# First attention of a two-layer gated block: sums over keys by a block of ones, the pair divided ahead of one 128-row output product

## The chip, the cores and the metric

The kernel runs on one core of a Trainium2 chip. The metric is the device time of one execution in microseconds (us), from start to end; of several runs the median is taken. The engines are named as in the profile: PE (TensorE, with PEld for its weight loads), DVE (VectorE), ACT (ScalarE), POOL (GpSimd) and SP (SyncE). A name like L713 is a line of the kernel before.

## The reference

Two layers, each an attention to a context of 77 rows and a feed-forward part. The change touches the first attention alone: queries come from the 2 x 1024 normalized rows of x (the latents), keys and values from the 77 rows of the context and from those rows themselves, 1101 keys in all, with 4 heads of 64.

```python
def _L0_xattn_ref(x, latents, mask, ...):        # x: the context, latents: layernorm of x
    xn, ln = layernorm(x, ...), layernorm(latents, ...)
    q = ln @ W_q
    kv = concatenate([xn @ W_kv, ln @ W_kv], axis=1)
    ...
    qn = rmsnorm(q, q_gamma) * SCALE
    kn = rmsnorm(k, k_gamma)
    sim = einsum('bhid,bhjd->bhij', qn, kn)
    sim = where(full_mask[:, None, None, :], sim, neg)
    attn = softmax(sim, axis=-1)
    out = einsum('bhij,bhjd->bhid', attn, v)
    out = out.transpose(0, 2, 1, 3).reshape(b, nl, INNER)
    return out @ W_out + b_out
...
x = x + tanh(g_xattn[0]) * _L0_xattn_ref(ctx_1024, _layernorm(x, axis=-1), mask_BxS2_bk0, ...)
x = x + tanh(g_ffn[0]) * _L0_ffn_ref(...)
x = x + tanh(g_xattn[1]) * _L1_xattn_ref(...)
x = x + tanh(g_ffn[1]) * _L1_ffn_ref(...)
```

## The kernel before

Every engine has its own program, written out by hand in `layers_kernel`; semaphores join them. The stages stand one after the other: weights of the second attention folded, the first projection, the first attention (97 to 407 us of the span), the spiking feed-forward part, the second attention, routing and experts. All data is 32-bit.

**Pairs and steps.** The first attention goes over 8 *pairs* (`PP`; 0 to 7), each two heads by 512 query rows of one batch: pairs 0 to 3 are batch 0, pairs 4 to 7 batch 1. A pair has 9 *steps* c, one for each chunk of 128 keys (the last of 77). In a step `pe_attend` puts out, in this order: `key_scores` (L713, L714: scores with keys as rows, for both heads, into banks 3 and 4), one `row_scores` of the *next* pair (L689, whose largest value DVE takes by `row_max`, L830), some small pieces, and `values` (L722) of those chunks that `CHUNK_OF_STEP` gives to the step. ACT takes the exponentials of the key scores into `EX`, a ring of four chunks (L1022). The row maxima of a pair are turned by `turn_shift` (L703) and copied by `keep_shift` (L849) into a row of the queries, so that the next pair's scores come out shifted.

**The end of a pair.** POOL adds the exponentials of the first six chunks (L986), DVE the others and both sums (`sum_first`, `sum_rest`, L858 to L866) into `sumD`. In step 1 of the next pair `sums` (L731) adds `sumD` over its 128 rows: eight products whose moving side is one column of ones, so that the sums of 128 queries come out on 128 rows, one column each. `reciprocals` (L870) inverts those 8 columns. ACT has copied the unscaled output to `OT`, 64 rows a head. `project_out` (L742), one half in step 2 and one in step 4, multiplies OT with W_out, head by head, since each head has its own divisor; `add_out` (L885) scales each head's product by its column and adds it to X, eight operations of 256 columns in a pair.

**Pieces.** While pairs 1 to 4 run, the projections of the other heads (two *units* of 9 items, first for pairs 4 and 5, then for pairs 6 and 7) are made beside them: `item` (L759), DVE's `square_sums` and `scale_heads` (L903, L914) with POOL's root between (L994), `turn_heads` (L768), ACT's copies and DVE's `low_parts_of` (L927, L930). The tables FIRST_AT, FIRST_TURNS (pairs 1 and 3), SECOND_AT, SECOND_TURNS (pairs 2 and 4), ROWS_AT and NORM_AT give each piece its step. What DVE does of an item or a turn beyond the square sums stands at the start of its next step. `keys_there` (step 0 of pairs 3 and 5) holds the next pair's row scores until the last piece of its unit is through.

**Spare banks.** All small products share banks 2, 6 and 7. `spare_uses` lists the uses in the order in which PE comes to them, and the k-th use takes bank k % 3, so a use waits until the use three places before it has been read:

```python
    def open_bank(pe, *use):
        k = order_of[use]
        if k >= 3:
            pe.wait_ge(bank_free[k % 3], k // 3)
        return SPARE[k % 3]
```

## Time and profile before

| what | value |
|---|---|
| median of 3 runs | 935.12 us (933.39 to 937.04) |
| profiled execution, its own time | 933.5 us |
| its span, first to last instruction | 931.1 us |
| mean granted clock of TensorE | 0.935 |
| busy over the span: PE, PEld, DVE | 845.8, 626.1, 607.6 us |
| busy over the span: ACT, POOL | 313.8, 372.8 us |

The profile is of one execution; its windows and starts count from its first instruction. A product of two 32-bit operands stands in the trace as two records (`x`). The granted clock is a share of the full one: 1.00 is 2.4 GHz, 0.50 is 1.2 GHz. A matmul's end is modelled, and the next begins before it; where a price matters, it is read from a run of like products. A wait put down to "issue" is one for which the profile shows no releaser. `DVEq L888` is the empty instruction by which `add_out` gives a bank free.

### The profile page before, as it was taken

To read this page: it belongs to the slowest core of one execution; us is meant where nothing else is said; L and a number is where in the kernel's file an instruction comes from. 1 tells how busy PE (TensorE), PEld (TensorE's weight loads), DVE (VectorE), ACT (ScalarE), POOL (GpSimd) and SP (SyncE) were. 2 spreads that over 40 slices of the span, in tenths; PEclk is the share of its full clock that TensorE was granted. 3 is DMA by queue.
4 is the path that set the end of the run, shared out by engine and by line. 5 is a ranking of instruction groups with operands and counts; after the bars stand their busy time and mean duration, and the time that the engine had idled before them with its cause. 6 is when DMAs were issued, how large, how long until landed. Compare 5 with 4: busy or idle time off the path is not lost.

```text
span 931.1 us, 13492 instructions
## 1 busy us (share of the span) xinstructions
PE 845.8 (91%) x4334; PEld 626.1 (67%) x4335; DVE 607.6 (65%) x1199; ACT 313.8 (34%) x703; POOL 372.8 (40%) x389
## 2 busy tenths in 40 slices
PE   6888799999999899969999799999997889999995
PEld 5455445555655555448888577777776779999994
DVE  5959676776677576359988688899886723333331
ACT  4557134543445233423444122333331022222220
POOL 4255555362556264524447044434443313222221
PEclk9999599998999799969999899999999799999999
DMA  8381000000000000045000650000000274555530
GB/s 304 119 313 49 1 1 0 1 1 1 1 0 1 1 0 1 2 147 211 0 0 1 205 167 8 12 12 12 13 11 18 77 262 159 175 188 188 167 85 2
DMA packets 32135, 67.88 MB, mean 73 GB/s; under 512 B 3161, under 2 KB 23095, under 8 KB 30999
## 3 DMA queue, kind: packets, MB, share of 16 engines
q1 hardware_dynamic: 28887, 56.63, 17.6%
q0 software_dynamic: 2624, 10.49, 3.7%
q8 instruction: 24, 0.39, 0.2%
q10 hardware_dynamic: 578, 0.18, 0.1%
q14 instruction: 22, 0.18, 0.1%
HBM read 55.20 MB, written 13.01 MB: 73 GB/s over the span
## 4 chain that ended last, share of the span: by engine, by line
PE 67%; DVE 18%; issue 7%; ACT 3%; POOL 2%; DMA 2%; DVEq 0%; SPq 0%; ACTq 0%; POOLq 0%
PE PS L2047 9%; PE PS L2035 8%; PE PS L1420 7%; PE PS L1438 6%; PE PS L722 6%; PE PS L1264 4%; PE PS L713 4%; PE PS L689 3%; DVE row_best L830 3%; PE PS L714 3%; PE PS L759 2%; PE PS L1422 2%; PE PS L731 2%; PE PS L742 2%; PE PS L1248 2%
## 5 line engine op out<-in xcount | busy, mean ns | idle before, releaser
L1022 ACT ACTIVATE EX<-PS 128x512 f32<-128x512 f32 x144 | 79.1, 594 | 139.7 <-PE PS L714 134.8
L830 DVE TENSOR_REDUCE row_best<-PS 128x1 f32<-128x1024 f32 x64 | 77.8, 1221 | 49.2 <-PE PS L689 48.9
L986 POOL TENSOR_TENSOR sumP<-sumP,EX 128x1024 f32<-128x1024 f32 x32 | 75.6, 2363 | 42.4 <-ACT EX L1022 41.8
L2035 PE MATMUL PS<-xeT,w 128*128 128x128 f32 x736 | 86.1, 275 | 3.6 <-DMA w<-in_L_ffn_W 2.6
L2035 PEld LDWEIGHTS PS<-xeT,w 128*128 128x128 f32 x736 | 85.6, 192 | 5.1 <-DMA w<-in_L_ffn_W 2.8
L2047 PE MATMUL PS<-w,heT 128*128 x368 | 83.3, 379 | 1.3 <-DVE oe L1977 1.3
L722 PE MATMUL PS<-EX,V 128*64 128x512 f32 (+1 forms) x288 | 75.9, 645 | 0.0
L2047 PEld LDWEIGHTS PS<-w,heT 128*128 128x128 f32 x368 | 68.1, 190 | 10.0 <-issue 1.7
L2074 POOL DMA_INDIRECT out<-oe,target x23 | 23.2, 1011 | 127.4 <-DVE oe L1977 127.4
L1438 PE MATMUL PS<-vw,pcT 128*128 128x256 f32 (+1 forms) x320 | 73.1, 383 | 1.2 <-ACT pcT L1630 1.2
L713 PE MATMUL PS<-QA,KA 100*128 100x512 f32 x144 | 71.3, 495 | 0.6 <-ACT EX L1022 0.6
L1438 PEld LDWEIGHTS PS<-vw,pcT 128*128 128x128 f32 (+1 forms) x320 | 59.6, 190 | 9.0 <-issue 1.3
L713 PEld LDWEIGHTS PS<-QA,KA 100*128 100x128 f32 x144 | 28.9, 200 | 49.7 <-issue 38.5
L714 PE MATMUL PS<-QB,KB 128*128 128x512 f32 x144 | 61.5, 427 | 0.0
L2007 ACT ACTIVATE heT<-PS,cols 128x128 f32<-128x128 f32 x92 | 26.2, 368 | 101.8 <-PE PS L2035 101.8
L1966 DVE TENSOR_SCALAR heT<-PS,cols 128x128 f32<-128x128 f32 x92 | 25.9, 344 | 52.7 <-PE PS L2035 52.7
L689 PE MATMUL PS<-KA,QA 65*128 65x512 f32 x128 | 49.5, 477 | 11.3 <-DVE row_best L830 5.3
L1311 POOL TENSOR_TENSOR square<-relu 128x512 f32<-128x512 f32 x32 | 38.0, 1196 | 33.9 <-ACT relu L1287 33.3
L1619 ACT ACTIVATE pc<-pc 128x462 f32<-128x462 f32 (+1 forms) x32 | 22.9, 717 | 81.2 <-DVE pc L1520 81.2
L1975 DVE TENSOR_TENSOR oe<-PS,b 128x256 f32<-128x256 f32 x23 | 9.8, 424 | 61.0 <-PE PS L2047 61.0
L1675 POOL TENSOR_TENSOR pc<-pc,sum 128x462 f32<-128x462 f32 x16 | 16.8, 1049 | 66.9 <-DVE sum L1528 66.9
L689 PEld LDWEIGHTS PS<-KA,QA 65*128 65x128 f32 x128 | 27.1, 228 | 24.5 <-DVE row_best L830 12.7
(292 smaller groups left out, 1793.7 us busy)
## 6 DMA issues: line engine op xcount, KB each, us to landing
w<-in_L_ffn_W SPq DMA_DIRECT2D x31, 1024.0 KB, 6.0
vw_rows<-vwn SPq DMA_DIRECT2D x2, 1232.0 KB
kwH_rows<-kwH SPq DMA_DIRECT2D x1, 2464.0 KB
kwL_rows<-kwL SPq DMA_DIRECT2D x1, 2464.0 KB
kwH<-kwH_rows POOLq DMA_DIRECT2D x1, 2464.0 KB, 10.4
kwL<-kwL_rows POOLq DMA_DIRECT2D x1, 2464.0 KB, 14.9
vw<-vw_rows SPq DMA_DIRECT2D x2, 1152.0 KB, 7.2
XR<-in_x SPq DMA_DIRECT2D x4, 512.0 KB, 13.5
```

The lines of the kernel that those rows point to most:

```text
L689: last = pe.matmul(PS[:, at + k0 // 512, 0:k1 - k0], QA[0:MASKROW + 1, g, h, s * P:s * P + P], KA[0:MASKROW + 1, h, k0:k1], start=True, st ...
L713: pe.matmul(out, KA[0:SHIFT + GT, h, cols], QA[0:SHIFT + GT, g, h, :], start=True, stop=False)
L714: pe.matmul(out, KB[:, h, cols], QB[:, g, h, :], start=False, stop=True).then_inc(st_done, 1)
L722: last = pe.matmul(PS[i * E0:i * E0 + E0, PV_AT, :], V[0:r, c, h, :], EX[0:r, (KT * n + c) % EB, i, :], start=c == 0, stop=c == KT - 1)
L830: dve.tensor_reduce(row_best[:, n % 2, t // GT, t % GT:t % GT + 1], PSf[:, 512 * at:512 * at + S], AX.X, ALU.max, negate=True).then_inc(ma ...
L986: pool.tensor_tensor(sumP[:], before, EX[:, (KT * n + c) % EB, :, :], ALU.add).then_inc(pool_summed, 1)
L1022: act.activation(EX[0:r, k % EB, i, :], PS[0:r, ST_AT + i, :], ACT.Exp).then_inc(exp_done, 1)
L1311: pool.tensor_tensor(square[:, c % 4, :], relu[:, c % 4, :], relu[:, c % 4, :], ALU.mult).then_inc(squared, 1)
L1420: pe.matmul(PS[:, 1 + i, 0:c1 - c0], z[:, p, k * P:k * P + P], w[:, k, b, c0:c1], start=w is kwH and z is zcH and k == 0, stop=False)
L1438: ins = pe.matmul(PS[:, 7, 0:D], pcT[0:r, c, :], vw[0:r, b, c, :], start=c == 0, stop=c == HC - 1)
L2035: last = pe.matmul(PS[:, 1 + 2 * p + c // 4, c % 4 * P:c % 4 * P + P], w1[:, u, k, c * P:c * P + P], xeT[:, p, k, :], start=k == 0, stop=k ...
L2047: last = pe.matmul(PS[:, 5 + p, 0:D], heT[:, p, c, :], w[:, ds(e * (FC * D) + c * D, D)], start=c == 0, stop=c == FC - 1)
```

## The change

The sums over keys: `sums` multiplies `sumD` (moving, 512 columns) by a 128 x 64 block of ones, one product a head, so that the sum of each query stands on all 64 rows of its head, the layout of OT. `reciprocals` inverts these 512 columns in two halves, one in step 1 behind the row maximum and one in step 2, and the sums' bank is free after the second; `scale_out` multiplies OT by them into `rl`. `project_out` takes both heads in one product of 128 rows (W_out lies as 2 blocks of 128 rows, loaded by one transfer), a half in step 3 and a half in step 5, into one bank each; `add_out` is one addition of 512 columns a half. The tables move pieces of pairs 2 and 4 to earlier steps, and the second `turn_shift` goes behind the first values of step 8.

```diff
-    onecol = att.take("onecol", [P, 1])
+    ones64 = att.take("ones64", [P, E0])
...
-    wout = att.take("wout", [P, H0, D])
+    wout = att.take("wout", [P, KC, D])
...
-    SECOND_AT = {0: (4,), 2: (5,), 3: (6,), 5: (7,), 6: (8,)}
+    SECOND_AT = {0: (4,), 1: (5,), 2: (6,), 4: (7,), 5: (8,)}
...
-    SECOND_TURNS = {1: (3,), 2: (4,), 4: (5,), 5: (6,), 7: (7,), 8: (8,)}
+    SECOND_TURNS = {1: (3,), 2: (4,), 3: (5,), 4: (6,), 6: (7,), 7: (8,)}
...
             k0 = open_bank(pe, "sum", n, 0)
             pe.wait_ge(dve_summed, 3 * n + 3)
             for i in range(2):
-                for s in range(GT):
-                    last = pe.matmul(PS[:, k0, i * GT + s:i * GT + s + 1],
-                                     sumD[:, i, s * P:s * P + P], onecol[:], start=True, stop=True)
+                last = pe.matmul(PS[i * E0:i * E0 + E0, k0, :], ones64[:], sumD[:, i, :], start=True, stop=True)
             last.then_inc(sum_done, 1)

         def project_out(n, half):
-            if half == 0:
-                pe.wait_ge(ot_ready, n + 1)
-            banks = [open_bank(pe, "out", n, 2 * half + i) for i in range(2)]
+            k0 = open_bank(pe, "out", n, half)
+            pe.wait_ge(out_scaled, n + 1)
             for s in (2 * half, 2 * half + 1):
-                for i, h in enumerate(heads_of(n)):
-                    lo = slice(i * E0, i * E0 + E0)
-                    last = pe.matmul(PS[:, banks[i], s % 2 * D:s % 2 * D + D], OT[lo, n % 2, s * P:s * P + P],
-                                     wout[lo, h, :], start=True, stop=True)
+                last = pe.matmul(PS[:, k0, s % 2 * D:s % 2 * D + D], rl[:, s * P:s * P + P], wout[:, n // 2 % 2, :],
+                                 start=True, stop=True)
             last.then_inc(proj_done, 1)
...
-                    if c in (5, 8):
-                        turn_shift(n + 1, (c - 5) // 3)
+                    if c == 5:
+                        turn_shift(n + 1, 0)
...
-                    if c == 2:
+                    if c == 3:
                         project_out(n - 1, 0)
-                    if c == 4:
+                    if c == 5:
                         project_out(n - 1, 1)
...
                 for done in CHUNK_OF_STEP.get(c, ()):
+                    if done == KT - 1 and n + 1 < PP:
+                        turn_shift(n + 1, 1)
                     values(n, done)
...
-        def reciprocals(n):
+        def reciprocals(n, half):
             dve.wait_ge(sum_done, n + 1)
-            bank_read(dve.reciprocal(rl[:, n % 2].rearrange("p i s -> p (i s)"),
-                                     PS[:, bank_of("sum", n, 0), 0:2 * GT]), "sum", n, 0)
+            if n > 0:
+                dve.wait_ge(proj_done, 2 * n)
+            w = slice(half * (GN // 2), half * (GN // 2) + GN // 2)
+            ins = dve.reciprocal(rl[:, w], PS[:, bank_of("sum", n, 0), w])
+            if half == 1:
+                bank_read(ins, "sum", n, 0)
+
+        def scale_out(n):
+            dve.wait_ge(ot_ready, n + 1)
+            wait_read(dve, "sum", n, 0)
+            dve.tensor_tensor(rl[:], OT[:, n % 2, :], rl[:], ALU.mult).then_inc(out_scaled, 1)
...
-            for i in range(2):
-                for s in (2 * half, 2 * half + 1):
-                    done = 2 * GT * n + GT * half + 2 * i + s % 2
-                    if done >= 2:
-                        dve.wait_ge(proj_added, done - 1)
-                    row = X[:, batch_of(n) * (S // P) + GT * group_of(n) + s, :]
-                    ins = dve.scalar_tensor_tensor(row, PS[:, bank_of("out", n, 2 * half + i), s % 2 * D:s % 2 * D + D],
-                                                   rl[:, n % 2, i, s:s + 1], row, ALU.mult, ALU.add).then_inc(proj_added, 1)
...
+            if n >= 2:
+                wait_read(dve, "out", n - 2, half)
+            at = batch_of(n) * (S // P) + GT * group_of(n) + 2 * half
+            rows = X[:, at:at + 2, :]
+            bank_read(dve.tensor_tensor(rows, PS[:, bank_of("out", n, half), :].rearrange("p (s d) -> p s d", d=D), rows,
+                                        ALU.add), "out", n, half)
...
                 if n > 0 and c == 1:
-                    reciprocals(n - 1)
+                    reciprocals(n - 1, 0)
                 if n > 0 and c == 2:
+                    reciprocals(n - 1, 1)
+                    scale_out(n - 1)
+                if n > 0 and c == 3:
                     add_out(n - 1, 0)
-                if n > 0 and c == 4:
+                if n > 0 and c == 5:
                     add_out(n - 1, 1)
...
-        for lo in (0, E0):
-            sp.dma_start(wout[lo:lo + E0], t["L0_xattn_W_out"].rearrange("(h e) n -> e h n", e=E0)).then_inc(wts_in, 16)
+        sp.dma_start(wout[:], t["L0_xattn_W_out"].rearrange("(r p) n -> p r n", p=P)).then_inc(wts_in, 16)
```

Three places show how the order moves. In the rows of the changed kernel the lines are its own: L714, L715 key scores, L690 row scores, L723 values, L764 turned heads, L755 items, L704 the turned shift, L738 the output product.

The first place is PE in steps 1 and 2 of pair 2, from the sums of pair 1 on. Before:

```order
L731 MATMUL PS<-onecol,sumD 128x1 x8
L768 MATMUL PS<-ident,qk 128x128 x4
L722 MATMUL PS<-EX,V 64x512 x2
L713 MATMUL PS<-QA,KA 128x512
L714 MATMUL PS<-QB,KB 128x512
L713 MATMUL PS<-QA,KA 128x512
L714 MATMUL PS<-QB,KB 128x512
L689 MATMUL PS<-KA,QA 128x512 x2
L742 MATMUL PS<-wout,OT 128x256 x4
L768 MATMUL PS<-ident,qk 128x128 x4
L759 MATMUL PS<-wqkv,lnT 128x384 x2
```

Now:

```order
L731 MATMUL PS<-sumD,ones 64x512 x2
L764 MATMUL PS<-ident,qk 128x128 x4
L755 MATMUL PS<-wqkv,lnT 128x384 x2
L723 MATMUL PS<-EX,V 64x512 x2
L714 MATMUL PS<-QA,KA 128x512
L715 MATMUL PS<-QB,KB 128x512
L714 MATMUL PS<-QA,KA 128x512
L715 MATMUL PS<-QB,KB 128x512
L690 MATMUL PS<-KA,QA 128x512 x2
L764 MATMUL PS<-ident,qk 128x128 x4
L755 MATMUL PS<-wqkv,lnT 128x384 x2
```

Item 5 has come from step 2 to step 1, item 6 from step 3 to step 2, and the output product has left step 2, so that the turn of item 4 (the second L764) follows the row scores of step 2 and stands three uses of a spare bank behind the sums.

The second place is DVE in the same steps, from the scaling of item 4's heads (`qk`, bracketed is what the instruction waits for) to the first add of before, and to the scaled output now. Before:

```order
L914 TENSOR_TENSOR qk<-PS,rrms 128x512 [waits v_ready,rrms_ready]
L830 TENSOR_REDUCE row_best<-PS 128x1 [waits s_done]
L870 RECIPROCAL rl<-PS 128x8 [waits sum_done]
L896 TENSOR_SCALAR Z<-ctxn,meanvar,rstd 128x256 [waits zT_done]
L927 SCALAR_TENSOR_TENSOR QB<-PS,cols,QB 64x2x128 [waits high_ready]
L930 SCALAR_TENSOR_TENSOR KB<-PS,cols,KB 64x2x128
L830 TENSOR_REDUCE row_best<-PS 128x1 [waits s_done]
L885 SCALAR_TENSOR_TENSOR XR<-PS,rl,XR 128x256 [waits bias_added,proj_added,bank_free2,proj_done]
```

Now:

```order
L916 TENSOR_TENSOR qk<-PS,rrms 128x512 [waits v_ready,rrms_ready]
L828 TENSOR_REDUCE row_best<-PS 128x1 [waits s_done]
L871 RECIPROCAL rl<-PS 128x256 [waits proj_done,sum_done]
L905 TENSOR_REDUCE ssum<-sq 128x4 [waits sq_ready]
L908 TENSOR_SCALAR rms<-ssum 128x4 [waits ssum_ready]
L929 SCALAR_TENSOR_TENSOR QB<-PS,cols,QB 64x2x128 [waits high_ready]
L932 SCALAR_TENSOR_TENSOR KB<-PS,cols,KB 64x2x128
L916 TENSOR_TENSOR qk<-PS,rrms 128x512 [waits v_ready,rrms_ready]
L828 TENSOR_REDUCE row_best<-PS 128x1 [waits s_done]
L871 RECIPROCAL rl<-PS 128x256 [waits proj_done,sum_done]
L878 TENSOR_TENSOR rl<-OT,rl 128x512 [waits bank_free0,ot_ready]
```

The first reciprocal stands ahead of item 5's square sums, the second behind the low parts, the scaling and the row maximum of step 2; the scaled output follows it.

The third place is PE in steps 7 and 8 of pair 2, from the turned heads of step 7 on. Before:

```order
L768 MATMUL PS<-ident,qk 128x128 x4
L722 MATMUL PS<-EX,V 64x512 x4
L713 MATMUL PS<-QA,KA 77x512
L714 MATMUL PS<-QB,KB 77x512
L713 MATMUL PS<-QA,KA 77x512
L714 MATMUL PS<-QB,KB 77x512
L703 MATMUL PS<-identr,NM 100x128
L768 MATMUL PS<-ident,qk 128x128 x2
L722 MATMUL PS<-EX,V 64x512 x4
```

Now:

```order
L764 MATMUL PS<-ident,qk 128x128 x2
L723 MATMUL PS<-EX,V 64x512 x4
L714 MATMUL PS<-QA,KA 77x512
L715 MATMUL PS<-QB,KB 77x512
L714 MATMUL PS<-QA,KA 77x512
L715 MATMUL PS<-QB,KB 77x512
L723 MATMUL PS<-EX,V 64x512 x2
L704 MATMUL PS<-identr,NM 100x128
L723 MATMUL PS<-EX,V 64x512 x2
```

The last turn (x2, that of item 8) has come from step 8 to step 7, and the turned shift (L703, now L704) has gone behind the first values of step 8.

## Rows read from the trace of the kernel before

**Rows 1.** Table of windows, the first attention: busy time of each engine, PEclk the granted clock.

```profile
core 0: us, PE busy (x) PEld busy (x) DVE busy (x) ACT busy (x) POOL busy (x), PEclk, DMA share, GB/s
97.00:407.00 310.00, 284.84 (x1198) 164.11 (x1198) 205.27 (x320) 116.85 (x248) 146.23 (x99) 0.89 0.00 1
```

**Rows 2.** Waits of TensorE, 97 to 410 us: us in total, times, longest us.

```profile
PE PS L689 <- issue: 4.7, 2, 2.4
...
PE PS L703 <- DVE NM L841: 4.4, 4, 1.9
PE PS L759 <- DVEq L888: 2.1, 4, 0.6
```

**Rows 3.** Timeline of TensorE, first attention: start us, us; L713 begins a step.

```profile
139.16 0.50 PE L713 MATMUL PS<-QA,KA 100*128 100x512 f32 x1
...
142.72 1.84 PE L731 MATMUL PS<-onecol,sumD 128*128 128x1 f32 x16
...
155.38 0.50 PE L713 MATMUL PS<-QA,KA 100*128 100x512 f32 x1
...
220.54 0.50 PE L713 MATMUL PS<-QA,KA 100*128 100x512 f32 x1
...
224.03 1.19 PE L689 MATMUL PS<-KA,QA 65*128 65x512 f32 x2 [2.29 <-issue]
...
242.71 0.50 PE L713 MATMUL PS<-QA,KA 100*128 100x512 f32 x1
...
305.74 0.50 PE L713 MATMUL PS<-QA,KA 100*128 100x512 f32 x1
...
326.77 0.50 PE L713 MATMUL PS<-QA,KA 100*128 100x512 f32 x1
...
342.55 0.50 PE L713 MATMUL PS<-QA,KA 100*128 100x512 f32 x1
...
357.52 0.50 PE L713 MATMUL PS<-QA,KA 100*128 100x512 f32 x1
```

**Rows 4.** Table of windows, stretches at the low clock; columns as in the first group.

```profile
145.30:148.60 3.30, 3.30 (x9) 1.55 (x6) 0.00 (x0) 1.39 (x3) 0.00 (x0) 0.50 0.00 0
...
223.80:237.40 13.60, 13.37 (x42) 9.29 (x42) 4.01 (x5) 2.39 (x4) 4.14 (x2) 0.50 0.01 1
...
309.10:322.70 13.60, 13.32 (x42) 9.29 (x42) 4.05 (x5) 2.39 (x4) 4.09 (x2) 0.50 0.00 1
...
377.40:380.70 3.30, 3.30 (x10) 1.34 (x7) 0.00 (x0) 0.66 (x2) 1.16 (x1) 0.50 0.00 0
```

**Rows 5.** Groups by line and shape, VectorE from 560 us on: busy us, mean ns.

```profile
L1528 DVE RECIPROCAL sum<-sum 128x6 f32<-128x6 f32 x13 | 2.5, 192 | 0.4
```

**Rows 6.** One source line: duration in ns, least, median, greatest.

```profile
L1814 DVE RECIPROCAL rtn<-rtn x1: 252/252/252, 727.4 to 727.4; 128x16 f32<-128x16 f32 x1
```

**Rows 7.** Timeline of TensorE: prices of products, x records.

```profile
149.18 1.13 PE L742 MATMUL PS<-wout,OT 64*128 64x256 f32 x8
...
348.43 1.08 PE L722 MATMUL PS<-EX,V 128*64 128x512 f32 x4
...
594.18 4.57 PE L1438 MATMUL PS<-vw,pcT 128*128 128x256 f32 x20
```

**Rows 8.** Groups by line and shape, VectorE, 90 to 560 us: busy us, mean ns.

```profile
L1361 DVE TENSOR_TENSOR hL<-square,hH 128x512 fp32r<-128x512 f32 x32 | 41.0, 1350 | 1.8 <-POOL square L1311 1.8
...
L914 DVE TENSOR_TENSOR qk<-PS,rrms 128x512 f32<-128x512 f32 x18 | 12.4, 691 | 10.9 <-POOL rrms L994 10.6
```

**Rows 9.** Timeline of VectorE, pair 2, step 1.

```profile
183.76 0.41 DVE L903 TENSOR_REDUCE ssum<-sq 128x4 f32<-128x256 f32 x1
...
185.56 0.69 DVE L914 TENSOR_TENSOR qk<-PS,rrms 128x512 f32<-128x512 f32 x1 [1.18 <-POOL rrms L994]
186.17 1.21 DVE L830 TENSOR_REDUCE row_best<-PS 128x1 f32<-128x1024 f32 x1
```

**Rows 10.** Timeline of TensorE, end of the attention.

```profile
399.00 1.92 PE L731 MATMUL PS<-onecol,sumD 128*128 128x1 f32 x16 [1.58 <-DVE sumD L866]
...
407.50 1.97 PE L1235 MATMUL PS<-ident,Z 128*128 128x128 f32 x8 [1.76 <-DVE XR L885]
```

More of the change, by code:

```diff
@@ L214, in layers_kernel @@
     rrms = att.take("rrms", [P, 2, 2 * H0])
-    rl = att.take("rl", [P, 2, 2, GT])
     project = Region(att.at)
@@ L225, in layers_kernel @@
     OT = att.take("OT", [P, 2, GN])
+    rl = att.take("rl", [P, GN])
     lnT2 = att.take("lnT2", [P, KC, KT * P])
@@ L336, in layers_kernel @@
     (ctx_done, shift_in, rows_set, s_done, max_ready, shift_done, shift_ready, st_done, exp_done, pv_done, pool_summed,
[L337 removed]
+     dve_summed, sum_done, rl_ready, ot_ready, proj_done, out_scaled) = sems(
          "ctx_done shift_in rows_set s_done max_ready shift_done shift_ready st_done exp_done pv_done pool_summed "
[L339 removed]
+         "dve_summed sum_done rl_ready ot_ready proj_done out_scaled")
     (fold_done, fold_read, fold_high, wfc_split) = sems(
@@ L428, in pool_norm @@
             pool.tensor_tensor(rs[:, i, 0:GT], rs[:, i, 0:GT], minus_half[:, 0:GT], ALU.pow).then_inc(root_out, 1)
-        pool.wait_ge(wts_in, 64)
+        pool.wait_ge(wts_in, 48)
         pool.wait_ge(tanh_ready, 1)
@@ L647, in spare_uses @@
                     yield "ctx", n + 1, c // 4
-                if n + 1 < PP and c in (5, 8):
-                    yield "shift", n + 1, (c - 5) // 3
+                if n + 1 < PP and c == 5:
+                    yield "shift", n + 1, 0
                 if n > 0 and c == 1:
                     yield "sum", n - 1, 0
-                if n > 0 and c in (2, 4):
-                    yield "out", n - 1, (c - 2) // 2 * 2
-                    yield "out", n - 1, (c - 2) // 2 * 2 + 1
+                if n > 0 and c in (3, 5):
+                    yield "out", n - 1, (c - 3) // 2
                 if (n, c) in ROWS_AT:
@@ L660, in spare_uses @@
                     yield "item", v, i
+                if n + 1 < PP and c == 8:
+                    yield "shift", n + 1, 1
         yield "sum", PP - 1, 0
-        for k in range(4):
-            yield "out", PP - 1, k
+        for half in range(2):
+            yield "out", PP - 1, half
     order_of = {use: k for k, use in enumerate(spare_uses())}
@@ L876, in add_out @@
             if half == 0:
-                wait_read(dve, "sum", n, 0)
                 dve.wait_ge(bias_added, BG * batch_of(n) + group_of(n) + 1)
-            for i in range(2):
-                for s in (2 * half, 2 * half + 1):
-                    done = 2 * GT * n + GT * half + 2 * i + s % 2
-                    if done >= 2:
-                        dve.wait_ge(proj_added, done - 1)
-                    row = X[:, batch_of(n) * (S // P) + GT * group_of(n) + s, :]
-                    ins = dve.scalar_tensor_tensor(row, PS[:, bank_of("out", n, 2 * half + i), s % 2 * D:s % 2 * D + D],
-                                                   rl[:, n % 2, i, s:s + 1], row, ALU.mult, ALU.add).then_inc(proj_added, 1)
-                    if s % 2 == 1:
-                        dve.engine_nop().then_inc(bank_free[order_of["out", n, 2 * half + i] % 3], 1)
+            if n >= 2:
[4 more added lines that the diff above has]
+                                        ALU.add), "out", n, half)
         def normalize_tiles(q):
@@ L971, in dve_attend @@
         ffn_z(dve, 0)
-        reciprocals(PP - 1)
+        reciprocals(PP - 1, 0)
+        reciprocals(PP - 1, 1)
+        scale_out(PP - 1)
         add_out(PP - 1, 0)
@@ L1220, in sp_refill @@
     def sp_refill(sp):
-        sp.wait_ge(proj_added, 2 * GT * PP)
+        wait_read(sp, "out", PP - 1, 1)
         for b in range(B):
@@ L1266, in group @@
                 last.then_inc(y_done, 1)
-        pe.wait_ge(proj_added, 2 * GT * PP)
+        wait_read(pe, "out", PP - 1, 1)
         pe.wait_ge(wfc_split, 4)
@@ L2107, in _ @@
         pool.memset(blocks[:], 0.0).then_inc(rows_set, 1)
-        pool.memset(onecol[:], 1.0)
+        pool.memset(ones64[:], 1.0)
         pool.memset(minus_half[:], -0.5).then_inc(ident_set, 1)
@@ L2122, in _ @@
         pool_root(pool, 1)
-        pool.wait_ge(proj_added, 2 * GT * PP)
+        wait_read(pool, "out", PP - 1, 1)
         pool_refill(pool)
@@ L2155, in _ @@
         pe.wait_ge(ident_set, 4)
-        pe.wait_ge(wts_in, 64)
+        pe.wait_ge(wts_in, 48)
         pe.wait_ge(ones_set, 4)
```

6 lines of the change are left out of this document (2 added, 4 removed).

## The prediction

> **What bounds the kernel now.** I read the table of windows first: in the first attention, from 97 to 407 us, TensorE is busy 285 of 310 us, VectorE 205, ScalarE 117, at a mean granted clock of 0.89 [rows 1]. So TensorE sets the pace there, in two ways that busy time hides: it runs in part at the lower of its two clock levels, and it stands still at a few places. The waits of TensorE name the places [rows 2]: row scores that wait for "issue" (4.7 us in two waits), the turned shift that waits for NM (4.4 us), and products that wait for a bank that the output adds free (2.1 us). The timeline of TensorE then gives the steps [rows 3]. From the start of pair 1 to its step 4 is 139.16 to 155.38, 16.2 us; the same tables of pieces in pair 3 take 220.54 to 242.71, 22.2 us. Pair 6 takes 342.55 to 357.52, 15.0 us; pair 5, also without pieces, 305.74 to 326.77, 21.0 us. Both long ones begin with the row scores of the next pair, which stood idle for 2.3 us (pair 3): they need the other two heads' keys, whose last piece was turned only in step 8, and VectorE makes its low part after the sums of the pair. After that idle time the granted clock fell to 0.50 (1.2 of 2.4 GHz) for 13.6 us, in pair 5 again [rows 4]. Five shorter stretches at 0.50, 3.3 us each (at 145, 186, 272, 350 and 377 us, the first and the last shown), each begin while or just after TensorE has done the sums over keys: 16 records of one column, 1.84 us [rows 3, 4].
>
> **The change, part by part.** Times are against the profiled execution, 933.5 us with a span of 931.1; the median of the runs shown, 935.1, is 1.6 above it.
>
> *Pieces in other steps.* The last turn of the second unit moves from step 8 to step 7. Its low part is then made ahead of the pair's sums, and nothing is left for the row scores of pairs 4 and 6 to wait for. Pair 3 then costs what pair 1 costs and pair 5 what pair 6 costs: (22.2 − 16.2) + (21.0 − 15.0) = **−12.0 us** [rows 3]. Of 6.0 each, 2.3 is the wait and 3.7 the clock. If the clock falls anyway, only 2 × 2.3 = 4.6 us comes: the lower end.
>
> *The sums.* Two products of 512 columns, whose heads use different columns of the array, as in the product with V: 4 records in 1.08 us [rows 7], less than 0.1 us of which is the end of the last. Against 1.84 I take 0.8 us saved in each of seven pairs (the eighth is in the tail): **−5.6**. The work is now of the same kind as the stages around it, which run at 1.00, so the five short falls should go. A stretch of 3.3 us at half speed costs at most 1.7, where TensorE alone sets the pace; part lies beside waits, so I take 0.8 each: **−4.0**, between 0 and −8.3.
>
> *The output product.* A half was 8 records in 1.13 us; four records of 128 rows cost 4/20 of 4.57 = 0.91 [rows 7]. 14 halves by 0.2: **−2.8**. The adds drop from eight to two and free their bank at once; the wait for them goes: **−2.1** [rows 2].
>
> *VectorE.* It gets 512 columns of reciprocal a pair in place of 8. The reciprocals of the trace lie on one line: 192 ns for 6 columns [rows 5], 252 for 16 [rows 6], so 6.0 ns a column above 156. So 256 columns take 156 + 1536 = 1.69 us, two 3.4 us. The Trainium skill (VectorE: DVE Perf Modes, "First, the fixed hardware budget") says that a reciprocal goes through an iterative divide with a repeat count of 8; at the 0.96 GHz of its "Specifications" that would be 8.3 ns a column, an estimate of 4.6 us a pair. The rows, at 6.0 ns, do not bear the 8 out, so the rows stand. The product with OT and each add are one operation of 512 columns, 0.69 us, or 1.35 where GpSimd works beside it in SBUF [rows 8]. In all 3.4 + 0.7 + 1.4 = 5.5 us a pair, more than the eight adds took. VectorE was idle for 105 of 310 us [rows 1], so its load does not set the end; its order does:
>
> *The new wait for the scaled output* (pairs 1, 3, 5, 6, 7). In step 3 TensorE now waits for reciprocal 1 and the product, 1.69 + 0.69 = 2.4 us after row maximum 2, behind which it has only row scores and the context scores, some 1.0 us. Idle 1.4 to 2.0 us (with the slower product); I take 1.7 × 5 = **+8.5**. Queued behind it are the values of chunks 1 and 2, for which ScalarE waits to refill EX. Bounds: 0 if TensorE comes late anyway, 10.
>
> *The bank of the sums* (pairs 2 and 4). The spare banks go round in threes, and in step 2 the turn of piece 4 is the third use after the sums: it waits until reciprocal 1 has read them. In the old trace VectorE ends row maximum 1 at 186.17 + 1.21 = 187.4 [rows 9]. From there to the end of reciprocal 1 it now has two reciprocals 3.4, a square sum 0.4, GpSimd's root 1.1 (the wait in front of the scaling), a scaling of heads 0.7 and row maximum 2, 1.2: 6.8 us, to 194.2 (two low parts lie beside the root). TensorE starts piece 5 when the heads of piece 4 are scaled, at 185.56 + 0.69 = 186.3, and then has a step's worth of products; a mean step of pair 6 is (15.0 − 1.8)/4 = 3.3 us [rows 3], so it is there at 189.6 and idle for 4.6 us. What stands behind has been brought forward and partly catches up, so I take half, 2.3 × 2 = **+4.6** (bounds 0 and 9.2), and a short fall of the clock after it, 1.7 × 2 = **+3.4**.
>
> *The shift's turn* goes behind the first values of step 8. That covers about half of the 4.4 us, but VectorE's copy of it, and so the pair's sums and the next row maximum behind it, come 0.7 us later in pairs without pieces (three times): I take the two as equal, **0**, within ±2.
>
> *The tail.* Sums at 399.0, next stage at 407.5 [rows 10]. New: 1.0 for the sums, 3.4 + 0.7 on VectorE, two product halves at the low clock 1.8 each, an add 0.7, some 0.2 of hand-over: 9.6 against 8.5, **+1.1**.
>
> The loads (one transfer of W_out in place of two), GpSimd's scaling of half as many columns and the larger memset lie in the start-up, where GpSimd waits anyway: 0; with that cover gone, under 2 us.
>
> Sum: −12.0 − 5.6 − 4.0 − 2.8 − 2.1 + 8.5 + 4.6 + 3.4 + 0 + 1.1 = −8.9, so 924.6; against the median's 1.6 I lean on the profiled execution and say **925 us**.
>
> **Rivals.** (1) *TensorE has slack where it now waits.* The new waits stand where it used to wait for row maxima and banks. Then half of the 8.5 goes, and the clock does not fall in pairs 2 and 4: −8.9 − 4.2 − 3.4 = −16.5, 917 us. For: row maxima already pace steps 1 to 3. Against: step 3 has little ahead of the product.
>
> (2) *The short falls are not the sums' doing*, but that of the idle time ahead; they stay (+4.0), and in pairs 2 and 4 the fall is a long one. A long one costs 3.7 + 0.8 = 4.5, so 2 × (4.5 − 1.7) = 5.6 more: −8.9 + 9.6, 934 us, no change. For: 2.3 us idle went ahead of both long falls. Against: the short ones follow the sums whatever went ahead of them.
>
> (3) *Slower: the wait for the scaled output lets the clock fall for long in every pair.* Place: step 3 of pairs 1, 3, 5, 6, 7 and step 2 of 2 and 4. Without falls the sum is −12.3; each long fall costs 4.5: three make +1.2, from the fourth pair on it is slower by over half a per cent, and all seven give +19.2, 953 us. For: the new idle of 1.4 to 4.6 us brackets the 2.3 of pair 3. Against: in pair 3 the sums came at once after it, and now work that kept 1.00 follows.
>
> (4) *A reciprocal of 256 columns costs more a column than one of 16.* Nothing in the rows shows it, reading PSUM could. At a third more, 1.2 us a pair on the path of seven pairs: +8.4, 933 us. The skill's page named above gives nearly this figure; the trace agrees only that a reciprocal is dear.
>
> **How the numbers follow.** Forecast 0.49, rival 1 0.24, rival 2 0.14, rival 3 0.10, rival 4 0.03. A measurement of this kernel can tell about 0.5% from no change, here 930.4 to 939.8. The forecast alone lies between 919 and 932 by its bounds, about a seventh of it within the 0.5%; with rival 1 faster has 0.70. Rivals 2 and 4 and that seventh give 0.19 for the same, rival 3 and a remnant 0.11 for slower. The range goes from 914 (rival 1 with the short falls at their full price) to 938, which takes in rivals 2 and 4 and leaves out most of rival 3.
>
> **What would show it.** Right: no idle time ahead of the row scores at the start of pairs 3 and 5, and no 0.50 there; sums of about 1 us; reciprocals near 1.69 us; TensorE idle before the output product in step 3 and, longest, before the turn in step 2 of pairs 2 and 4. Wrong: the clock at 0.50 for long in pairs 1, 6 or 7; reciprocals above 2 us; or a step 8 that grows because the shift's copy comes too late for the next pair's first scores.

## The result and the profile after

| | before | changed |
|---|---|---|
| median | 934.03 us (930.38 to 937.04, 15 runs) | 939.34 us (937.44 to 942.12, 15 runs) |
| ratio | | 1.006, 95% interval 1.0045 to 1.0075 |
| span of the profiled execution | 931.1 us | 936.0 us |
| PE, DVE busy over the span | 845.8, 607.6 us | 832.0, 626.0 us |

The changed kernel is slower by 0.6%: on the other side of the forecast and outside its range. PE does 13.8 us less work, and the whole takes 5 us longer, so PE stands idle more. The table of windows over the stretch of [rows 1] shows it: PE is busy 267.56 us in place of 284.84, at a granted clock of 0.91 in place of 0.89, and VectorE 221.97 in place of 205.27. The changed kernel's attention goes on to 413.5 us; up to there PE is busy 271.31 us.

```profile
core 0: us, PE busy (x) PEld busy (x) DVE busy (x) ACT busy (x) POOL busy (x), PEclk, DMA share, GB/s
97.00:407.00 310.00, 267.56 (x1030) 141.70 (x1030) 221.97 (x285) 116.44 (x248) 146.55 (x99) 0.91 0.00 1
```

The line numbers of the changed kernel: L714 first product of a step, L690 row scores, L731 sums, L738 output product, L755 piece ("item"), L764 turn of heads, L871 reciprocal, L878 scaling of the output, L889 add, L932 low part, L993 GpSimd's running add. The waits of PE after, 105 to 415 us, answer to [rows 2] (us in total, times, longest):

```profile
PE PS L738 <- DVE rl L878: 14.7, 6, 4.4
PE PS L690 <- DVE row_best L828: 7.9, 14, 1.7
PE PS L764 <- DVE rl L871: 6.3, 2, 3.2
PE PS L755 <- DVE KB L932: 4.6, 2, 2.3
PE PS L738 <- DVE KB L932: 3.2, 4, 1.5
PE PS L704 <- DVE NM L839: 1.9, 1, 1.9
```

Row scores waiting for "issue" are gone, as forecast, and the shift's wait fell from 4.4 to 1.9 us, which stand ahead of pair 0. New are the scaled output (14.7, of which 4.4 in the tail) and the bank of the sums ahead of L764 (6.3), both forecast, and two that were not: items that wait for a low part (L755, 4.6 us) and output products that wait for one (L738, 3.2 us). Waits for a row maximum, from 105 us on, grew from 4.8 to 7.9 us.

From the step starts, the lengths of the pairs in the two profiled executions:

| us | pair 1 | 2 | 3 | 4 | 5 | 6 | 7, to step 8 | step 8 to next stage |
|---|---|---|---|---|---|---|---|---|
| before | 40.1 | 41.3 | 43.1 | 42.1 | 36.8 | 30.1 | 21.7 | 13.1 |
| changed | 38.6 | 46.1 | 35.1 | 45.9 | 36.4 | 34.8 | 22.4 | 14.6 |
| difference | −1.5 | +4.8 | −8.1 | +3.8 | −0.4 | +4.7 | +0.7 | +1.5 |

Two rows of PE's timeline answer to pair 3 in [rows 3]: the row scores follow at once, and step 4 begins 14.7 us after the pair, where it was 22.2.

```profile
225.44 0.63 PE L690 MATMUL PS<-KA,QA 65*128 65x512 f32 x2
...
239.06 0.50 PE L714 MATMUL PS<-QA,KA 100*128 100x512 f32 x1
```

Pair 3 gains the 6.0 us that were forecast for its keys and 2 us more. Pair 5 was to gain as much and gains nothing, pair 6 loses, and pairs 2 and 4 lose more than the forecast gave them. The timeline of PE has the places. In pair 2, PE waits ahead of an item in step 0 and of the turn in step 2 (pair 4: 2.32 at 263.44 and 3.14 at 276.57):

```profile
182.25 2.31 PE L755 MATMUL PS<-wqkv,lnT 128*128 128x384 f32 x4 [2.31 <-DVE KB L932]
...
195.47 0.66 PE L764 MATMUL PS<-ident,qk 128*128 128x128 f32 x4 [3.16 <-DVE rl L871]
```

In or behind each of these four waits the granted clock fell to 0.50, for 3.4 us each, at the last for 6.8.

And ahead of the output product in pairs 1, 3, 5, 6 and 7:

```profile
152.15 1.10 PE L738 MATMUL PS<-wout,rl 128*128 128x256 f32 x4 [0.25 <-DVE rl L878]
...
236.17 1.10 PE L738 MATMUL PS<-wout,rl 128*128 128x256 f32 x4 [0.81 <-DVE rl L878]
...
320.28 2.05 PE L738 MATMUL PS<-wout,rl 128*128 128x256 f32 x4 [3.46 <-DVE rl L878]
...
355.53 2.04 PE L738 MATMUL PS<-wout,rl 128*128 128x256 f32 x4 [3.47 <-DVE rl L878]
...
386.12 1.10 PE L738 MATMUL PS<-wout,rl 128*128 128x256 f32 x4 [2.35 <-DVE rl L878]
```

The wait is under a microsecond in pairs 1 and 3 and over two in pairs 5 to 7. In pairs 5 and 6 the records double in length, 2.05 against 1.10 us: after the idle time the granted clock was 0.50. The table of windows, after:

```profile
319.50:326.30 6.80, 6.02 (x13) 2.38 (x14) 3.01 (x5) 0.00 (x0) 0.09 (x1) 0.50 0.00 0
353.60:360.40 6.80, 4.87 (x12) 1.95 (x12) 4.16 (x5) 0.00 (x0) 1.24 (x1) 0.50 0.00 0
```

Why those pairs? The timeline of pair 6 around the scaling, with GpSimd:

```profile
349.99 4.85 POOL L993 TENSOR_TENSOR sumP<-sumP,EX 128x1024 f32<-128x1024 f32 x2 [2.30 <-ACT EX L1029]
350.82 1.75 DVE L871 RECIPROCAL rl<-PS 128x256 f32<-128x256 f32 x1
...
352.68 2.71 DVE L878 TENSOR_TENSOR rl<-OT,rl 128x512 f32<-128x512 f32 x1
```

The scaling takes 0.69 us in pairs 1 to 4 and in the tail, but 2.71, 2.71 and 2.18 in pairs 5, 6 and 7. There it starts while one of GpSimd's adds runs, and in all three pairs it ends 0.55 us after that add; in pair 6 this is the second of the two shown, which end at 354.84. Both its inputs, OT and rl, lie in SBUF. The Trainium skill (SBUF — State Buffer, "SBUF: two separate sides") says that a VectorE instruction with two SBUF inputs and a GpSimd instruction that reads SBUF exclude each other at a shared pair of ports for a whole instruction. The trace agrees, with the 0.55 us in all three pairs. The kernel before had shown such a hold too, in a row that the prediction did not use: the tiny NM (4 columns, two inputs in SBUF) by its line, least, median and greatest ns, and the case of 2.19 us beside GpSimd. It begins in the first of four adds that follow one another without a gap, and ends 0.03 us after the last.

```profile
L841 DVE TENSOR_TENSOR NM<-row_best,ctx_best x13: 161/164/2193, 135.2 to 369.2; 128x4 fp32r<-128x4 f32 x13
```

```profile
300.45 2.78 POOL L1005 TENSOR_TENSOR XR<-XR,boutb 128x256 f32<-128x256 f32 x4
301.07 2.19 DVE L841 TENSOR_TENSOR NM<-row_best,ctx_best 128x4 fp32r<-128x4 f32 x1
```

### The profile page after: what moved, and what is told of

It is laid out like the page before. It is cut to its first block, busy times and chain, and to the rows that moved or that the text cites. A ratio compares the mean times of both kernels' runs of the same rounds, so it can differ in the third digit from the quotient of the medians.

```text
span 936.0 us, 13120 instructions
## 1 busy us (share of the span) xinstructions
PE 832.0 (89%) x4174; PEld 605.9 (65%) x4175; DVE 626.0 (67%) x1167; ACT 313.5 (33%) x703; POOL 372.6 (40%) x389
## 4 chain that ended last, share of the span: by engine, by line
PE 65%; DVE 20%; issue 7%; ACT 3%; POOL 3%; DMA 2%; DVEq 0%; SPq 0%; ACTq 0%; POOLq 0%
PE PS L2053 9%; PE PS L2041 8%; PE PS L1444 7%; PE PS L1426 7%; PE PS L723 6%; PE PS L1270 4%; DVE row_best L828 3%; PE PS L714 3%; PE PS L690 2%; PE PS L1254 2%; PE PS L755 2%; PE PS L738 2%; PE PS L715 2%; PE PS L1428 2%; DVE hL L1367 2%
## 5 line engine op out<-in xcount | busy, mean ns | idle before, releaser
L993 POOL TENSOR_TENSOR sumP<-sumP,EX 128x1024 f32<-128x1024 f32 x32 | 75.8, 2368 | 42.6 <-ACT EX L1029 41.5
L723 PE MATMUL PS<-EX,V 128*64 128x512 f32 (+1 forms) x288 | 75.8, 636 | 0.0
L714 PE MATMUL PS<-QA,KA 100*128 100x512 f32 x144 | 70.5, 489 | 1.5 <-ACT EX L1029 1.2
L714 PEld LDWEIGHTS PS<-QA,KA 100*128 100x128 f32 x144 | 28.0, 195 | 49.2 <-issue 30.4
L715 PE MATMUL PS<-QB,KB 128*128 128x512 f32 x144 | 59.9, 416 | 0.0
L690 PE MATMUL PS<-KA,QA 65*128 65x512 f32 x128 | 47.2, 458 | 9.6 <-DVE row_best L828 8.3
L1367 DVE TENSOR_TENSOR hL<-square,hH 128x512 fp32r<-128x512 f32 x32 | 40.9, 1345 | 1.7 <-POOL square L1317 1.7
## 6 DMA issues: line engine op xcount, KB each, us to landing
kwL<-kwL_rows POOLq DMA_DIRECT2D x1, 2464.0 KB, 14.5
```

The lines of the kernel that those rows point to most:

```text
L690: last = pe.matmul(PS[:, at + k0 // 512, 0:k1 - k0], QA[0:MASKROW + 1, g, h, s * P:s * P + P], KA[0:MASKROW + 1, h, k0:k1], start=True, st ...
L714: pe.matmul(out, KA[0:SHIFT + GT, h, cols], QA[0:SHIFT + GT, g, h, :], start=True, stop=False)
L715: pe.matmul(out, KB[:, h, cols], QB[:, g, h, :], start=False, stop=True).then_inc(st_done, 1)
L723: last = pe.matmul(PS[i * E0:i * E0 + E0, PV_AT, :], V[0:r, c, h, :], EX[0:r, (KT * n + c) % EB, i, :], start=c == 0, stop=c == KT - 1)
L993: pool.tensor_tensor(sumP[:], before, EX[:, (KT * n + c) % EB, :, :], ALU.add).then_inc(pool_summed, 1)
L1367: dve.tensor_tensor(hL[:, c, :], square[:, c % 4, :], hH[:, c, :].bitcast(F32), ALU.subtract).then_inc(h_low, 1)
```

## The experiments

Three theories are tested. Theory A: the held scaling, with the fall of the clock behind it, costs pairs 5 to 7 what the sums and keys bring there. Theory A2: the second reciprocal comes too late for the bank of the sums. Theory S: the moved turn of the shift makes the items of step 0 wait. Ratios are to the kernel before on the same chip; a gain against the changed kernel is the difference of the ratios times 934 us.

**1. The scaling reads the sums' bank** (theory A). The reciprocals are written back into that bank, and the scaling frees it; the waits are changed to match.

```
-  ins = dve.reciprocal(rl[:, w], PS[:, bank_of("sum", n, 0), w])
+  sums = PS[:, bank_of("sum", n, 0), w]
+  dve.reciprocal(sums, sums).then_inc(rl_ready, 1)
...
-  dve.tensor_tensor(rl[:], OT[:, n % 2, :], rl[:], ALU.mult).then_inc(out_scaled, 1)
+  bank_read(dve.tensor_tensor(rl[:], OT[:, n % 2, :], PS[:, bank_of("sum", n, 0), :], ALU.mult), "sum", n, 0)
```

> The changed kernel with one thing other: the reciprocals are written back into the bank of the sums and the scaling reads that bank and OT, so that it has one input in SBUF and one in PSUM instead of two in SBUF; nothing else moves. Theory A (the scaling is held by GpSimd's running add when both its inputs are in SBUF): the scaling lasts about 0.7 us in every pair, in pairs 5 to 7 too (2.70, 2.71 and 2.18 us there in the changed kernel), the low-clock stretches of 6.8 us in pairs 5 and 6 shorten to 3.4 or go, pairs 5 and 6 lose about 4 us each and pair 7 about 1, pairs 1 to 4 stay: 929 to 933 us where the changed kernel has 939, so no slower than before. Rival B (GpSimd's add slows any work of VectorE at that place): the scaling still takes over 2 us, 937 to 941. Rival C (the scaling shortens but the clock falls come from something else): only the 2 us of each of three pairs or less, 934 to 937, and the stretches of 6.8 us stay.

Measured: 931.75 us, ratio 0.999 (0.997 to 1.0011), 6.5 us less than the changed kernel. The scaling by its line, and the place in pair 6:

```profile
L877 DVE TENSOR_TENSOR rl<-OT,PS x8: 686/689/689, 151.0 to 403.6; 128x512 f32<-128x512 f32 x8
```

```profile
349.69 4.85 POOL L992 TENSOR_TENSOR sumP<-sumP,EX 128x1024 f32<-128x1024 f32 x2 [2.30 <-ACT EX L1028]
...
352.37 0.69 DVE L877 TENSOR_TENSOR rl<-OT,PS 128x512 f32<-128x512 f32 x1
...
353.20 1.99 PE L738 MATMUL PS<-wout,rl 128*128 128x256 f32 x4 [1.45 <-DVE rl L877]
```

The scaling starts at the same point of the same two adds and takes 0.69 us. PE's wait drops from 3.47 to 1.45, the stretch at 0.50 behind it from 6.8 to 3.4, and pairs 5, 6 and 7 by 3.2, 2.7 and 1.5 us. Theory A stands; rivals B and C fall. Given back: the bank is now freed by the scaling, and the turn of heads in pairs 2 and 4 waits 9.0 us in two waits (6.3 in the changed kernel); pair 1 has a stretch of 3.4 us at 0.50 that the changed kernel had not, and is 2.0 longer. Of the 6.4 us between the two profiled spans, 4.6 lie in the attention and before it; 1.8 lie behind it, where the two programs are alike.

**2. Both reciprocals in step 1** (theory A2).

```
   if n > 0 and c == 1:
       reciprocals(n - 1, 0)
+      reciprocals(n - 1, 1)
   if n > 0 and c == 2:
-      reciprocals(n - 1, 1)
       scale_out(n - 1)
```

> The changed kernel with both reciprocals in step 1, one behind the other, instead of one in step 1 and one in step 2; the scaling still two inputs in SBUF and in step 2. Theory A2 (in pairs 2 and 4 the turn of heads 4 waits 3.2 us for the bank of the sums, which the second reciprocal frees): that wait shortens to 1.5 us or less and the low-clock stretch behind it goes or stays short, 2 to 3 us gained in each of the two pairs; the scaling comes some 1 us earlier in the others and still meets GpSimd's add in pairs 5 to 7, so those gain little: 933 to 937. Rival (the bank is free in time anyway, and the loss in pairs 2 and 4 comes from the heads' bank in step 0 alone): 938 to 941. Other rival: the row maxima of step 2 are late behind two reciprocals in a row, and the row scores of step 3 wait: 940 to 944.

Measured: 923.88 us, ratio 0.9898 (0.9873 to 0.9923), 15 us less than the changed kernel: the largest effect of one line, and below the times that the theory and both its rivals gave. The waits of PE:

```profile
PE PS L690 <- DVE row_best L828: 9.6, 14, 1.7
PE PS L738 <- DVE rl L878: 7.1, 3, 4.3
PE PS L755 <- DVE KB L932: 5.6, 4, 2.3
PE PS L738 <- DVE KB L932: 5.6, 6, 1.6
```

The wait for the bank of the sums is gone (0.2 us is left); row maxima behind two reciprocals cost 1.7 us more. Pairs 2 and 4 gain only 0.9 and 1.3 us, since the waits of items in step 0 stay and the clock still falls there. What was not expected: pairs 5 and 6 gain 3.7 and 3.2. No reciprocal stands between row maximum 2 and the scaling any more, and the scaling is held by the first of GpSimd's two adds, not the second; in pair 6:

```profile
342.51 5.12 POOL L993 TENSOR_TENSOR sumP<-sumP,EX 128x1024 f32<-128x1024 f32 x2 [2.27 <-ACT EX L1029]
...
344.23 1.19 DVE L878 TENSOR_TENSOR rl<-OT,rl 128x512 f32<-128x512 f32 x1
```

The scaling is now held in pairs 1 to 4 too (1.95, 1.13, 1.20 and 1.12 us), where PE hardly waits for it, and pair 7 is 1.6 us longer, with a fall of 3.4 us behind its wait. A2 holds for the wait; most of the gain lies elsewhere. The profiled execution, 927.06 us, was the longest of this kernel's six, so the pairs in it show less than the median's 15.

**3. Both edits.**

> The two edits together: both reciprocals in step 1 and written into the bank of the sums, the scaling reads it there. The bank then is freed by the scaling and not by the second reciprocal. Theories A and A2 together: pairs 5 to 7 gain as with the first edit (6 to 10 us in all), pairs 2 and 4 gain as with the second less the 0.7 us of the scaling: 925 to 930. If the gains are one and the same (a fall that is avoided at one place comes at another): no better than the first edit alone, 929 to 935.

Measured: 924.14 us, ratio 0.9909 (0.9885 to 0.9933), the same as the second edit alone. Pairs 5 to 7 are shorter still (31.6, 31.3 and 20.9 us), but pairs 2 and 4 take 46.9 and 45.1: the bank again, two waits of 8.5 us in sum. What the one place gains the other gives back.

**4. The second shift's turn back in its place** (theory S), in PE's order as shown and in the order of the spare banks alike.

```
-  if c == 5:
-      turn_shift(n + 1, 0)
+  if c in (5, 8):
+      turn_shift(n + 1, (c - 5) // 3)
...
-  if done == KT - 1 and n + 1 < PP:
-      turn_shift(n + 1, 1)
```

> The changed kernel with the turn of the second shift back at its place before the change, in step 8 ahead of the turns of heads, in PE's order and in the order of the spare banks. Theory S (moving it behind the others made items 4 wait 2.3 us in step 0 of pairs 2 and 4 for a bank that VectorE frees behind the last sums): those two waits go, the wait for the shift's own input (4.4 us over all pairs before the change) comes back, the short falls of the clock behind them in pairs 2 and 4 go: 933 to 938. Rival (the bank is late by the low parts alone, wherever the shift stands): waits of item 4 stay, and the shift's wait is added: 941 to 945.

Measured: 930.79 us, ratio 0.9983 (0.9967 to 1.0), 7.2 us less than the changed kernel, and below the expected 933 to 938. The item in step 0 of pair 2:

```profile
178.83 1.45 PE L753 MATMUL PS<-wqkv,lnT 128*128 128x384 f32 x4
```

It has no idle time ahead of it, and that of pair 4 has none either. With the shift behind the others, the order of the spare banks is heads 2, item 3, shift, item 4: item 4 has the bank of heads 2, and VectorE makes the low part that frees it behind the sums of the pair. With the shift ahead it is shift, heads 2, item 3, item 4 (with the turn of rows ahead of heads 2 in pair 1), and that bank was free long before. Theory S stands for the two waits. It does not account for the whole gain: pairs 2 and 4 shorten by 1.3 us each, 1.5 of the 6.1 us between the profiled spans lie behind the attention, where the two programs are alike, and the rest is spread over the other pairs. The wait for the bank of the sums, which comes later in pairs 2 and 4, grows from 6.3 to 7.5 us.

**5. The tables alone, in the kernel before.** Edit: `SECOND_AT`, `SECOND_TURNS`, `ROWS_AT` and `NORM_AT` as in the change.

> The kernel before with nothing but the tables of the change (the pieces of keys and of rows in other steps); sums, reciprocals, output product and shift as before. Theory of the prediction (the pieces alone bring 12 us, by the waits for keys at the start of pairs 3, 5 and 6 and the falls of the clock there): pair 3 loses some 6 to 8 us, the other pairs stay within 2 us, 920 to 925 where before has 933. Rival (pairs 2 and 4 lose what pair 3 gains, since the items moved into them press on the spare banks): pairs 2 and 4 are 2 us or more longer, as in the changed kernel, and the total is 929 to 934.

Measured: 927.16 us, ratio 0.9931 (0.9902 to 0.996): 6.4 us, half of the 12, and above the expected 920 to 925. In pair 3 the row scores no longer wait for "issue", and yet:

```profile
222.79 0.73 PE L689 MATMUL PS<-KA,QA 65*128 65x512 f32 x2 [0.77 <-DVE row_best L830]
223.36 2.49 PE L731 MATMUL PS<-onecol,sumD 128*128 128x1 f32 x16
```

```profile
224.40:234.60 10.20, 10.20 (x29) 5.84 (x29) 3.49 (x7) 1.19 (x2) 3.18 (x2) 0.50 0.00 0
```

That wait is gone, 0.77 us for a row maximum stand in its place, and the clock falls all the same, now during the one-column sums, for 10.2 us; in pair 5 it does too. Pairs 3 and 5 gain 2.8 and 2.3 us, little more than the wait itself. Pairs 2 and 4 are 42.5 and 40.8 us, about as before: the tables do not cause their loss.

**6. The sums, scaling, product and moved shift without the tables.** Edit: the four tables of before in the changed kernel.

> The changed kernel with the four tables of before: the new sums, the scaling, the product and the moved shift alone. The tables alone have given about 5.5 us to the kernel before. Theory (the parts add up; the loss of pairs 2 and 4 and the held scaling belong to the sums and the product, not to the tables): some 5 us slower than the changed kernel, 942 to 948 us where before has 933; the scaling takes over 2 us in at least two of pairs 5 to 7. Rival (the tables bring the spare banks into trouble in pairs 2 and 4): pairs 2 and 4 return to 42 us each, and the total is 934 to 938.

Measured: 947.75 us, ratio 1.0146 (1.0109 to 1.0182). The scaling takes 2.71, 2.70 and 2.18 us in pairs 5 to 7; pairs 2 and 4 take 45.7 and 44.8. So this half of the change costs 13.6 us as it was placed, and the tables bring 8.0 on top of it.

**7. The one-column products put back** ahead of the new sums, into the bank that these write over; this kernel holds work that neither of the others does.

> The changed kernel with the eight one-column products of before put back ahead of the new sums of each pair, into the same bank, where the new sums write over them; the result is that of the changed kernel and the time holds work that neither kernel does. Theory N (the one-column products are what the clock fell for behind the sums in pairs 1, 3, 6 and 7 of the kernel before): the stretches of 3.4 us at half clock come back one after the sums of each of pairs 1, 3 and 7, where the changed kernel has none; 0.8 us more per pair of eight and 1 to 2 us per fall: 10 to 15 us more than the changed kernel, 947 to 953. Rival (the falls come from the idle time around the sums): only the work itself, 6 to 8 us, 943 to 946, no new fall in pairs 1, 3 and 7.

Measured: 961.14 us, ratio 1.0306 (1.0262 to 1.035), 23 us more than the changed kernel. The expectation was wrong in the price of the work: 0.8 us is what the change saves, the eight products themselves cost 1.84 [rows 3], 14.7 in eight pairs. Right behind the sums the clock falls again in pair 1, and in pairs 5 and 6, which the expectation did not name; in pair 3 it does not, and the fall in pair 7 (6.8 us) begins in the wait for the scaled output. In pair 1:

```profile
144.77 1.89 PE L732 MATMUL PS<-ones,sumD 128*128 128x1 f32 x16
146.59 1.97 PE L734 MATMUL PS<-sumD,ones 128*64 128x512 f32 x4
```

The new sums take 1.97 us there, not 1.08, at 0.50. Pair 5, in the changed kernel and here, with the stretch behind it here:

```profile
310.20 0.72 PE L690 MATMUL PS<-KA,QA 65*128 65x512 f32 x2 [1.67 <-DVE row_best L828]
310.85 1.08 PE L731 MATMUL PS<-sumD,ones 128*64 128x512 f32 x4
```

```profile
319.67 0.73 PE L690 MATMUL PS<-KA,QA 65*128 65x512 f32 x2 [1.68 <-DVE row_best L831]
320.24 3.17 PE L732 MATMUL PS<-ones,sumD 128*128 128x1 f32 x16
```

```profile
320.50:327.30 6.80, 6.80 (x24) 3.94 (x24) 2.92 (x2) 0.00 (x0) 0.70 (x1) 0.50 0.00 0
```

The idle time ahead is the same, 1.67 and 1.68 us (in pair 1 it is 0.96 in both kernels, in pair 6 0.97), and only with the one-column products does the clock fall. So the forecast's reason for the short falls is borne out in pairs 1, 5 and 6. Why the clock holds behind the sums of pairs 3 and 7 stays open.

**8. Early reciprocals and the shift back** (edits 2 and 4).

> The changed kernel with both reciprocals in step 1 and the second shift's turn back ahead of the turns of heads in step 8. The two edits alone gave 15 and 8.5 us against the changed kernel. If they act at different places (the bank of the sums and the scaling on the one hand, the wait of item 4 in step 0 of pairs 2 and 4 on the other), the wait of item 4 goes, pairs 2 and 4 lose 2 to 3 us each against the first edit alone, 917 to 921 where before has 933. Rival (each edit only moves where the clock falls, so that the gains overlap): 922 to 925, no better than the first edit alone.

Measured: 920.24 us, ratio 0.9861 (0.9823 to 0.9899), 18.6 us less than the changed kernel, of 22 by the two alone. Pair 4 drops to 40.7 us with no fall of the clock; pair 2 has one fall, of 6.8 us, and 44.4.

**9. The same, with the scaling from the bank for the outputs of the fifth pair and later**, where no turn of heads waits for that bank.

> As the kernel with both of these edits, and for the outputs of the fifth pair and later (those scaled in pairs 5 to 7 and the tail) the reciprocals stay in the bank of the sums and the scaling reads it there, with one input in SBUF. Theory A (the scaling is held by GpSimd's add in pairs 5 to 7 when both inputs are in SBUF): the scaling falls from over 2 us to 0.7 in each of these, pairs 5 to 7 and the tail lose 1 to 3 us each against the kernel without this part, 2 to 5 us in all: 913 to 918. Rival (the early reciprocals already take the scaling out of the way of the output product): no difference beyond 1.5 us.

Measured: 915.05 us, ratio 0.9808 (0.9764 to 0.9851): 5.2 us below experiment 8 by the medians. The scaling takes 0.67 to 0.69 us in pairs 5 to 7 (2.07, 1.19 and 2.18 in experiment 8), and these pairs shorten by 1.2, 1.6 and 3.2 us. Pair 6 now runs without the wait ahead of L739 and at full clock:

```profile
336.05 4.85 POOL L1003 TENSOR_TENSOR sumP<-sumP,EX 128x1024 f32<-128x1024 f32 x2 [2.14 <-ACT EX L1039]
...
337.77 0.67 DVE L885 TENSOR_TENSOR rl<-OT,PS 128x512 f32<-128x512 f32 x1
...
338.84 1.11 PE L739 MATMUL PS<-wout,rl 128*128 128x256 f32 x4
```

This version beats both kernels: 1.9% under the kernel before, 2.5% under the changed one.

**10. The tail's scaling in halves** on top of experiment 9.

> The kernel with both edits and the bank-read scaling of the fifth pair and later (915 us), and in the tail the scaling in two halves, each behind its own reciprocal, the first half of the product waiting for the first alone. PE waits 4.3 us there for the scaled output; the first half comes one reciprocal (1.69 us) and half a scaling (0.34 us) earlier, the second no earlier than one half of the product: 1.5 to 2.5 us gained, 912 to 914. Rival (the tail is bound by the adds of VectorE and the statistics of the first tile behind them): within 0.5 us of the kernel without it.

Measured: 915.04 us, ratio 0.9785 (0.9745 to 0.9824), no different from experiment 9 by the medians, where 1.5 to 2.5 us were expected. The end of step 8 to the next stage shortens by 1.1 us (14.3 to 13.2), since the second half of the product still follows the second reciprocal. The profiled span is 1.3 us longer. Up to the tail the two programs do the same, and yet pair 2 took 44.5 us in experiment 9 and 41.6 here, where the clock did not fall; pair 0 is 1.4 longer here, and pair 6, which ran at full clock there, has 3.4 us at 0.50 and is 1.6 longer. A difference of 3 us in one pair of one profile can be the clock alone.

## Why the prediction was wrong

The sum was −8.9 and the result is +5.6 (0.6% of 934): 14.5 us apart. Experiments 5 and 6 split it: the pieces bring 8.0 in the changed kernel, not 12.0 (4.0 of the miss), and all the rest costs 13.6, not 3.1 (10.5 of the miss).

**The new wait for the scaled output** is the step that failed most. The time was nearly right, 10.3 us idle in the five pairs against 8.5, but not where: 0.25 and 0.81 in pairs 1 and 3, 3.46, 3.47 and 2.35 in pairs 5 to 7. "0.69 us, or 1.35 where GpSimd works beside it" took GpSimd as a slowdown, from a mean over a line [rows 8]. The same line by its least, median and greatest ns in the kernel before shows what the mean mixes:

```profile
L1361 DVE TENSOR_TENSOR hL<-square,hH x32: 677/1523/2514, 419.4 to 504.0; 128x512 fp32r<-128x512 f32 x32
```

It took 0.68 us with GpSimd idle, nearly always 1.52 beside it and once 2.51. In the changed kernel it is a hold until GpSimd's instruction ends: 2.71 us. And the term had no price for the clock behind its idle time, 6.8 us at 0.50 in each of pairs 5 and 6; rival 3 had the clock, not the hold. Removing the hold alone gave 6.5 us.

**"Pair 5 costs what pair 6 costs"** came near as a likeness (36.4 and 34.8 us) and was wrong as a gain, because the change lengthened pair 6 itself by 4.7. The step took a pair of the old kernel as the price of one in the new. "Pair 3 costs what pair 1 costs" was right (−8.1 us, with the sums' part). The lower end, that the clock falls anyway, is what the tables alone did in pairs 3 and 5.

**The shift's turn, "0, within ±2"**, was not free: putting it back gave 7.2 us. The profiles show 2.6 of it in the pairs with the two waits; that the rest is theirs is not shown. The prediction counted PE's and VectorE's order and left out the order of the spare banks, which it had followed for the sums a paragraph earlier.

**The bank of the sums**: place and wait were right, 3.2 us idle in each of pairs 2 and 4 against 2.3 taken, within the bounds. The pairs grew by 4.8 and 3.8 with the wait in step 0 on top, and a second fall of the clock; without that wait they are 1.3 us shorter each (experiment 4).

**Smaller terms.** The output product, "−2.8", brought nothing that shows: at full clock a half takes 1.08 to 1.13 us, where 0.91 was forecast and 1.13 measured before [rows 7]. The waits for banks that the adds free went, as "−2.1" has it, but output products now wait 3.2 us for low parts. And the waits for row maxima, put at nothing, are 3.1 us longer; which of VectorE's new work makes them so is not shown.

**Right**: the reciprocal (1695 to 1758 ns against 1.69 us) and the adds by their lines, the sums (1.08 us), the tail (+1.5 against +1.1). By line, and for the tail PE's timeline, which answers to [rows 10]:

```profile
L871 DVE RECIPROCAL rl<-PS x16: 1695/1748/1758, 145.3 to 406.3; 128x256 f32<-128x256 f32 x16
```

```profile
L889 DVE TENSOR_TENSOR XR<-PS,XR x16: 676/692/692, 156.1 to 412.8; 128x512 f32<-128x512 f32 x16
```

```profile
403.54 1.08 PE L731 MATMUL PS<-sumD,ones 128*64 128x512 f32 x4 [1.58 <-DVE sumD L864]
408.97 3.75 PE L738 MATMUL PS<-wout,rl 128*128 128x256 f32 x8 [4.35 <-DVE rl L878]
413.51 0.90 PE L1241 MATMUL PS<-ident,Z 128*128 128x128 f32 x3 [0.79 <-DVE XR L889]
```

The falls right after the sums in pairs 1, 6 and 7 went, as forecast; others came, after the new waits, one of them in pair 6, for 6.8 us, which the prediction had named as a sign of being wrong. The longest waits were to stand before the turn in pairs 2 and 4; they stand before the output product, 3.47 against 3.16 us.

**The rivals.** Rival 3 named the right side: the wait lets the clock fall. It happened in pairs 5 and 6 by this wait and in 2 and 4 by the banks, not in all, and for 3.4 or 6.8 us, not 13.6. Rival 4 is refuted by the reciprocals, rival 1 by the 10.3 us. Rival 2, that the short falls are the idle time's doing, is refuted in pairs 1, 5 and 6 by experiment 7 and stays open for pairs 3 and 7. The chances do not add up as stated: by their own parts faster has 0.66 and the same 0.24, not 0.70 and 0.19. That the sums and the product lose by their place and not by their arithmetic, experiments 2 and 9 show: well placed, with the shift back and the later scalings from the bank, they bring 11.5 us on top of the tables (the ratios 0.9931 and 0.9808).
